# A step's order on TensorE in a linear-attention kernel: state inputs and weighted values right behind the projections, scores last, and the PSUM banks that go with it

## The reference

```python
h = _layernorm(x) * (1 + ca) + sa
q = elu(h @ Wq) + 1; k = elu(h @ Wk) + 1; v = h @ Wv      # 16 heads of 64
a = sigmoid(h @ Wa + ba + 2.0)
# per head, along the 2048 tokens:
S = a_t * S + k_t (outer) v_t;  z = a_t * z + k_t
out_t = (q_t . S) / (q_t . z + eps)
x = x + ga * (out @ Wo)
h = _layernorm(x) * (1 + cb) + sb
x = x + gb * experts(h)                                   # top 2 of 8, softmax weights
```

## Time and profile before

| | |
|---|---|
| median of 3 runs | 3618.65 us (3607.57 to 3626.08) |
| profiled execution | 3621.35 us, span 3619.6 us |
| granted TensorE clock, mean | 0.983 |
| PE busy | 3264.2 us, 90%, 51114 instructions |
| PEld busy | 2783.3 us, 77%, 51114 instructions |
| DVE busy | 2613.1 us, 72% |
| ACT busy | 1754.8 us, 48% |
| POOL busy | 1226.6 us, 34% |
| last scan of the attention phase (L915) | 2678.1 us |

### The profile page before, as it was taken

One profiled execution on the slowest core, in us unless ns is written; L12 is line 12 of the kernel. 1 busy time (PEld: TensorE's weight loads), 2 busy tenths in 40 slices (PEclk: granted clock), 3 DMA queues, 4 the chain that ended last, 5 costly groups with the idle time before them and its releaser, 6 DMA issues. The chain is left out here.

```text
span 3619.6 us, 129713 instructions
## 1 busy us (share of the span) xinstructions
PE 3264.2 (90%) x51114; PEld 2783.3 (77%) x51114; DVE 2613.1 (72%) x6866; ACT 1754.8 (48%) x4365; POOL 1226.6 (34%) x1057
## 2 busy tenths in 40 slices
PE   6898999999998998899999989989987999999998
PEld 5777777778787777777787777778775777777777
DVE  5676767666767767676666677767757888888887
ACT  4565656555665665555555666556542111111211
POOL 3333333343443333333333433333321222222222
PEclk9999999999999999999999999999998999999999
DMA  4222222222222222222222222222212111111110
GB/s 138 68 73 71 76 71 70 73 67 73 76 87 72 68 74 74 67 73 73 67 73 68 77 83 73 71 71 75 67 51 77 42 36 42 42 36 36 48 36 24
DMA packets 158631, 238.73 MB, mean 66 GB/s; under 512 B 30232, under 2 KB 82504, under 8 KB 157768
## 3 DMA queue, kind: packets, MB, share of 16 engines
q1 hardware_dynamic: 158024, 230.33, 19.8%
HBM read 194.58 MB, written 35.67 MB: 64 GB/s over the span
## 5 line engine op out<-in xcount | busy, mean ns | idle before, releaser
L442 POOL TENSOR_TENSOR oT_lo<-oT,oT_hi 128x512 fp32r<-128x512 f32 x256 | 332.0, 1297 | 1491.4 <-ACT oT_hi L526 1464.8
L543 ACT ACTIVATE kd_sb<-bank_scores,decay 128x64 f32<-128x64 f32 x2048 | 446.9, 329 | 655.0 <-PE bank_scores L741 652.6
L896 DVE SCALAR_TENSOR_TENSOR s_mid<-s_mid,lam_bc,bank_nums 128x65 f32<-128x65 f32 x1280 | 361.5, 282 | 46.9 <-DVE s_mid L896 1.4
L450 POOL TENSOR_TENSOR qs_sb<-lam_bc,qk_sb 128x512 f32<-128x512 f32 x256 | 333.9, 1304 | 157.1 <-PE bank_nums L725 119.5
L896 DVE SCALAR_TENSOR_TENSOR s_mid<-carry,lam_bc,bank_nums 128x65 f32<-128x65 f32 x256 | 72.3, 282 | 430.4 <-PE bank_dense L732 428.8
L741 PE MATMUL bank_scores<-qk_sb 64*64 64x128 f32 x8192 | 346.1, 274 | 29.5 <-issue 29.4
L508 ACT ACTIVATE qk_sb<-bank 128x512 f32<-128x512 f32 x512 | 318.0, 621 | 38.5 <-PE bank L582 21.3
L510 ACT ACTIVATE qk_sb<-qk_sb 128x512 f32<-128x512 f32 x512 | 324.2, 633 | 16.3
L915 DVE TENSOR_TENSOR_SCAN decay<-a_bc,eye 128x512 f32<-128x512 f32 x256 | 315.6, 1233 | 21.8 <-DMA a_bc<-rows_dram 21.8
L525 ACT ACTIVATE oT<-bank 128x512 f32<-128x512 f32 x256 | 153.1, 598 | 297.7 <-PE bank L707 297.1
L1247 DVE SCALAR_TENSOR_TENSOR acc<-bank_scores,comb,acc 128x256 f32<-128x256 f32 x512 | 230.7, 477 | 78.4 <-PE bank_scores L1161 77.5
(11 more groups left out here) (214 smaller groups left out, 9650.4 us busy)
## 6 DMA issues: line engine op xcount, KB each, us to landing
a_bc<-rows_dram SPq DMA_DIRECT2D x512, 128.0 KB, 2.9
lam_bc<-rows_dram SPq DMA_DIRECT2D x512, 128.0 KB, 2.9
x_in<-in_L_attn_x_dram SPq DMA_DIRECT2D x32, 512.0 KB, 6.3
x_res<-in_L_attn_x_dram SPq DMA_DIRECT2D x32, 512.0 KB, 3.9
x_dram<-x_res SPq DMA_DIRECT2D x32, 512.0 KB, 3.4
x<-x_dram SPq DMA_DIRECT2D x32, 512.0 KB, 3.3
out_dram<-x SPq DMA_DIRECT2D x32, 512.0 KB, 2.9
ew_raw<-in_L_ffn_expert_W_dram SPq DMA_DIRECT2D x8, 256.0 KB, 6.0
```

The costliest lines, as they stand in the source:

```text
L442: pool.tensor_tensor(oT_lo[:, u, :], oT32[:, :], oT_hi[:, u, :].bitcast(F32), ALU.subtract).then_inc(oT_lo_ready, 1)
L450: pool.tensor_tensor(qs_sb[:, na, :], lam_bc[na][:, :], q_sb, ALU.mult).then_inc(qs_ready, 1)
L543: ins = act.activation(kd_sb[:, t, hd * DH:(hd + 1) * DH], KTR[:, hd, t * CK:(t + 1) * CK], ACT.Copy, scale=decay[:, hd, t, CK - 1:CK])
L896: dve.scalar_tensor_tensor(dst, src, lam_bc[nb][:, (ch + 1) * CK - 1:(ch + 1) * CK], U[ch], ALU.mult, ALU.add).then_inc(state_step, 1)
```

## The change

**TensorE's order.** Behind the projections now stand inter, then the state inputs of all eight chunks in one piece, then the products of weighted scores and values, then the output's transposes (at u = 0 behind the dense jobs), then the dense jobs, and at the end the keys and scores of all eight chunks in one piece.

**Banks.** The state inputs of even chunks go to bank K, those of odd chunks to EXTRA's first bank. The output's transposes go to the first bank of SCORES (at u = 0 to DENSE), the h job's to DENSE and SCORES' second bank, both wo jobs to Q. So the state inputs wait for k_sb, the k projection for the state chain of the step before, and the scores for the copies of the transposed output.

**The other engines.** VectorE's state chain stands before the decay scan. ScalarE copies the transposed output before the dense evacuation (not at u = 0). GpSimd makes qs_sb before oT_lo. The dense jobs move: h from u = 1 to u = 0, wo behind it, v jobs a place forward or back; h_low goes from u = 1 to u = 0, the layer norm's application from u = 7 and 0 to u = 6 and 7, its statistics start at u = 2.

```diff
-DENSE_JOBS = {(0, 0): ("wo", -1, 1), (0, 1): ("v", 0, 5), (1, 0): ("v", 0, 6), (1, 1): ("h", 1, 0), (2, 0): ("v", 0, 7),
+DENSE_JOBS = {(0, 0): ("h", 1, 0), (0, 1): ("wo", -1, 1), (1, 0): ("v", 0, 6), (1, 1): ("v", 0, 7), (2, 0): ("v", 1, 0),
...
-        U_REST, DENSE = EXTRA[:, 0, :], EXTRA[:, 1, :]
+        U_ODD, DENSE = EXTRA[:, 0, :], EXTRA[:, 1, :]
-        HT = [U_REST, Q]
+        HT = [DENSE, SCORES[:, 1, :]]
+        U = [(K, U_ODD)[ch % 2][:, ch // 2 * VW:(ch // 2 + 1) * VW] for ch in range(NCK)]
+        def o_bank(u):
+            return SCORES[:, 0, :] if u else DENSE
...
 # GpSimd
-                if exists(T):
-                    pool.wait_ge(oT32_ready, n + 1)
-                    pool.wait_ge(oT_hi_ready, n + 1)
-                    pool.tensor_tensor(oT_lo[:, u, :], oT32[:, :], oT_hi[:, u, :].bitcast(F32), ALU.subtract).then_inc(oT_lo_ready, 1)
                     pool.tensor_tensor(qs_sb[:, na, :], lam_bc[na][:, :], q_sb, ALU.mult).then_inc(qs_ready, 1)
+                if u == 0 and exists(T + 1):
+                    for kt in range(KT):
+                        h_low(T + 1, 1 - s, kt)
+                if exists(T):
+                    pool.wait_ge(oT32_ready, n + 1)
+                    pool.wait_ge(oT_hi_ready, n + 1)
+                    pool.tensor_tensor(oT_lo[:, u, :], oT32[:, :], oT_hi[:, u, :].bitcast(F32), ALU.subtract).then_inc(oT_lo_ready, 1)
...
 # TensorE, step
-                    after(pe, oT_hi_ready, a - 3)
+                    after(pe, state_step, (a - 1) * NCK)
                     project(Ta, sa, pa, "wk", K, k_ps)
...
                 if exists(Tb):
+                    if exists(Ta):
+                        pe.wait_ge(k_ready, a + 1)
                     pe.wait_ge(kd_ready, b + 1)
...
-                    entering((NCK - 1,), u_last_ps)
+                    for ch in range(NCK):
+                        for hd in range(2):
+                            half, t = place(hd, ch)
+                            mm = pe.matmul(U[ch][rows[hd], :], kd_sb[rows[half], t, rows[hd]], v_sb[rows[half], t, v_col(pb, hd), :],
+                                           start=True, stop=True)
+                    mm.then_inc(u_ps, 1)
...
+                def transpose_o():
+                    if exists(T):
+                        if u:
+                            after(pe, kd_ready, free)
+                            after(pe, p_ready, free)
...
+                        after(pe, oT_hi_ready, n)
+                        pe.wait_ge(o_ready, n + 1)
+                        for t in range(NCH):
+                            mm = pe.transpose(o_bank(u)[:, t * CH:(t + 1) * CH], o_sb[:, t, :], ident[:, :])
+                        mm.then_inc(oT_ps, 1)
...
 # VectorE, step
+                if exists(Tb):
+                    chain(Tb, sb_, pb, b)
+                if exists(Ta):
                     after(dve, p_ready, a)
                     dve.wait_ge(a_loaded[na], (Ta * (PAIRS // 2) + pa // 2 + 1) * 32)
                     dve.tensor_tensor_scan(decay[:, :, :, :].rearrange("p h t i -> p (h t i)"), a_bc[na][:, :],
...
-                if exists(Tb):
-                    chain(Tb, sb_, pb, b)
```

More of the change, by code:

```diff
@@ L450, in step @@
                     pool.tensor_tensor(qs_sb[:, na, :], lam_bc[na][:, :], q_sb, ALU.mult).then_inc(qs_ready, 1)
-                if u == 7 and exists(T + 2):
+                if u == 0 and exists(T + 1):
[5 more added lines that the diff above has]
+                    pool.tensor_tensor(oT_lo[:, u, :], oT32[:, :], oT_hi[:, u, :].bitcast(F32), ALU.subtract).then_inc(oT_lo_ready, 1)
+                if u == 6 and exists(T + 2):
                     reciprocal_deviation(T + 2)
                     ln_apply(T + 2, (0, 1))
-                if u == 0 and exists(T + 1) and not leads(T):
-                    ln_apply(T + 1, (2, 3))
-                if u == 1 and exists(T + 1):
-                    for kt in range(KT):
-                        h_low(T + 1, 1 - s, kt)
+                if u == 7 and exists(T + 2):
+                    ln_apply(T + 2, (2, 3))
                 if leads(T) and u == 4:
@@ L601, in q_bank_free @@
                     pe.wait_ge(lam_row_ready, T + 2)
[L602 to L603 removed]
             def h_job(T):
[L606 removed]
+                after(pe, v_ready, T * 8 - 2)
+                after(pe, kd_ready, T * PAIRS - 5)
+                after(pe, p_ready, T * PAIRS - 5)
                 pe.wait_ge(xn_ready, T + 1)
@@ L633, in v_job @@
                 n = T * 8 + half * NCH + t
-                dst = Q if half == 1 and t == 1 else DENSE
+                dst = Q if half == 1 and t == 3 else DENSE
                 if half == 1 and t == 2:
-                    after(pe, wo_scaled, T * 2)
+                    pe.wait_ge(oT_hi_ready, T * PAIRS + 1)
+                    if exists(T + 1):
+                        pe.wait_ge(h32_ready, T * 2 + 3)
                 after(pe, v_ready, n)
@@ L687, in step @@
                 rows = [slice(i * CK, (i + 1) * CK) for i in range(2)]
+                free = a if exists(Ta) or not isinstance(Ta, int) else max(0, min(a, NG * PAIRS))
                 if exists(Ta):
@@ new lines, in step @@
+                if u:
+                    transpose_o()
+                dense_job(T, s, u, 0)
+                if dense_at(T, s, u, 1)[0]:
+                    if exists(Ta):
+                        pe.wait_ge(q_ready, a + 1)
+                    else:
+                        q_bank_free(T, u)
+                dense_job(T, s, u, 1)
+                if not u:
+                    transpose_o()
+                if exists(Ta):
+                    pe.wait_ge(k_ready, a + 1)
+                    pe.wait_ge(q_ready, a + 1)
+                    after(pe, kd_ready, a)
+                    after(pe, p_ready, a)
+                    if u and exists(T):
+                        pe.wait_ge(oT_hi_ready, n + 1)
+                    if u == 0 and exists(T + 1):
+                        pe.wait_ge(h32_ready, T * 2 + 4)
+                    if isinstance(Ta, int) and a == 0:
+                        pe.wait_ge(eye_ready, 1)
+                    pe.sem_inc(inputs_seen)
+                    for ch in range(NCK):
+                        eye_q = qk_sb[:, 0:2 * (ch + 1) * CK].rearrange("p (x i) -> p x i", x=2)[:, :, 0:CK]
+                        for hd in range(2):
+                            half, t = place(hd, ch)
+                            mm = pe.matmul(KTR_S[rows[half], hd, :, t, :], k_sb[rows[hd], ch * CK:(ch + 1) * CK], eye_q[rows[hd], :, :],
+                                           start=True, stop=True)
+                    mm.then_inc(s_ps, 1)
```

110 lines of the change are left out of this document (34 added, 76 removed).

## The result

| | before | after |
|---|---|---|
| median | 3619.9 us (3607.57 to 3626.08, 4 runs) | 3723.03 us (3713.13 to 3723.27, 4 runs) |
| ratio to before | | 1.0283, 95% interval 1.0264 to 1.0302 |
| profiled span | 3619.6 us | 3721.1 us |
| 28 groups in the middle | 2328.8 us | 2404.9 us |

The change costs 103 us or 2.8%. The sign and the mechanism were forecast; the size was not: 56 us. The measured time lies outside the forecast's own range (3645 to 3710) and inside the wide one (3600 to 3740).

What follows compares the result with a forecast made beforehand. TensorE's order was taken as the bound, losing waits and gaps. New waits 8.7, tile changes 1.9, removed wait -4.8, gaps -3.3, clock -0.7 gave +1.8 us per group: 3677 us, own range 3645 to 3710, 8 in 10 3600 to 3740.

Steps and rivals of the forecast that it cites:

- 8.7: TensorE's entering chunks waiting for k_sb: these waits together were to add 8.7 us per group.
- light step: Step with one v job (u = 4, 5, 6): 8.14 us before, forecast near 9.2 when steady.
- the meeting: VectorE's scan meets GpSimd's oT_lo and ends 1.07 us after it; loop from kd to kd 9.22 us.
- Rival 4: No change: the meeting happens in part of the steps, or a delay hides at u = 3 and 4; 3621 us, chance 0.12.
- rival 1: Faster: scan and oT_lo do not meet, loop 8.6 us, waits 5.2, sum -1.7 per group; 3568 us, chance 0.16.
- Rival 3: Slower: VectorE's clamp is caught by GpSimd's qs, loop 10.0 us in half of some five steps; 3736 us, chance 0.11.
- the term -3.3: Gaps on issue in TensorE's 64x64 runs: 3.3 of 3.5 us per group go, as shorter runs outlast code packets.
- rival 2: Slower: TensorE's gaps on issue stay; with half of 3.5 us left, sum 3.4 per group, 3727 us, chance 0.11.
- the sum of +1.8 us per group: All terms together: 8.7 + 1.9 - 4.8 - 3.3 - 0.7; over 31 groups +56 us.
- -0.7: Projections' share of the granted clock and shorter gaps on TensorE: about 1, half hidden in new waits, -0.7 us per group.
- two more changes of tile size: One more stretch of 64x64 tiles on TensorE: 0.35 us per step, less about 0.1; +1.9 us per group.

Runs made afterwards that it cites:

- e2: The changed kernel, but GpSimd's oT_lo also waits for the decay scan of the same step, so the two never run at once; 3600.92 us, ratio 0.9943.
- e1: The changed kernel with VectorE's order alone put back: decay scan ahead of the eight state updates; 3698.45 us, ratio 1.0217.
- e9: e7 with the transposes and the dense job ahead of inter at u = 3, 4, 5 and 7; 3505.61 us, ratio 0.9688.
- e7: e5 and e3 together, decay scan at the start of VectorE's step, k's projection no longer waiting for the state updates; 3496.97 us, ratio 0.9661.
- e3: The changed kernel, but the v job that goes to bank Q does not wait for the other v job's copy; 3688.40 us, ratio 1.0184.
- e4: The changed kernel with the edits of e2 and e3 together; 3568.59 us, ratio 0.9864.
- e5: The changed kernel with state inputs back in their earlier banks, seven chunks' behind the products, without the wait for k_sb; 3575.60 us, ratio 0.9875.

## Why the prediction was right in sign and mechanism, and half too small

**Right.** The wait of the transposes is gone and the entering chunks wait for k_sb; the medians are 0.27, 0.26, 0.26 us at u = 0 to 2, then 1.63, 0.43, 1.42, 2.03 and 1.31 (forecast 0.27 three times, 1.9, 1.1, 1.4, 2.0, 1.4, which add up to 8.6 and not to 8.7). At u = 4 the missing 0.6 is PE's wait for lam_row, which stands ahead of it in the same step. The light step u = 5 takes 9.35 us, forecast 9.2. The scan meets oT_lo in 209 steps and ends 1.08 behind it in each (1.076 to 1.087), forecast 1.07 from one event in the earlier trace rows; e2, which takes the meeting away, is 122 us faster. Rival 4, that it meets in part of the steps only or hides, is refuted by this too. The forecast's rival 1, the same kernel without the meeting, was to give 3568; e2 gives 3601, and its u = 1 still has the 0.94 us below. The Trainium skill (SBUF — State Buffer, section "SBUF: two separate sides") calls the two engines' common port pair an exclusive lock in which the second waits for the whole instruction, and gives about 115 ns from the lock's release to the end for a DMA of GpSimd's that had waited for VectorE; the trace agrees with the lock in both directions (scan behind oT_lo, in e1 qs behind the scan), and has 1.08 us from the first's end to the second's, of the 1.215 or 1.29 that the second takes alone: most of it runs only then.

Rival 3 (clamp caught by qs) is refuted for the changed kernel: 303 to 310 ns in all 120 clamps, qs 0.16 behind. It is what e1 shows: 1220 ns in all 120 clamps, and 10.0 us steps, the length that the rival had.

The gaps on issue are gone (5.4 us in 7 of them left), as the term -3.3 had it, and with them rival 2's condition. That the rivals' 3727 and 3736 lie nearer to the measured 3723 than the forecast is chance. The reason given for the term is not confirmed. For it speaks that all 63 gaps over 0.6 us among the small matmuls of the kernel before (28 groups) end 1.19 to 1.57 us (median 1.36) after a code packet has landed, worked out from the DMA records, and that these packets start 0.4 to 1.6 us ahead of the gap but for one, 0.1 behind its start, all of them inside the run of small matmuls. Packets come every 7.4 us (median), so a fixed distance in all 63 is hardly chance. Three of them, us:

```
packet starts  packet landed  PE stops  PE resumes  resumes behind packet
338.75         340.11         339.51    341.55      1.44
422.88         424.14         423.88    425.59      1.45
451.19         452.14         452.82    453.44      1.30
```

So they are most likely waits for code. Against the run's length as the whole cause stand three counts: in runs of 128 at u = 4 and 5 e9 has 3 gaps over 0.6 us where the kernel before has 17; the kernel before has none at u = 0, 1 and 7, whose runs are as long, and 24 at u = 2; and e7 has 10 at u = 3 and 4 in and behind runs of 96. Where the packet boundaries fall in the code differs from kernel to kernel, and I can't move them at will; that stays open.

**Wrong: the sum of +1.8 us per group, which was 2.7 in the middle groups, and more at the start.** What it left out:

- *The v_ready wait at u = 1.* "u = 0 has h and wo and u = 1 a second v, which hide the loop". They do, but the second v job, into another bank, kept the wait for the copy of the first: 0.69 us idle, 0.94 in the step, x 31 = 29 us. e3 measures 35. The forecast counted the job and not its wait.
- *The clock.* "The projections' share of the granted clock of 0.99" was the only place where the forecast spoke of it, as a gain and a part of its -0.7. The gain did not come. Worked out from the clock records of both traces, TensorE runs at 1.2 GHz for 30.7 us of the 28 groups in the kernel before and for 30.7 us in the changed one; only the place is another. Before, these stretches stand behind gaps on issue (seven of 1.8 to 2.5 us, one of 3.5). In the changed kernel u = 6 waits 2.03 us for k_sb, and in 7 of 28 groups the step then takes 11.3 to 11.7 us, against 9.9. Two such waits, and the 3.2 us behind each:

```profile
310.60 0.36 PE L734 MATMUL bank<-v_sb,kd_sb 64*64 64x65 f32 x2 [2.02 <-DVE qk_sb L918]
```

```profile
396.52 0.27 PE L734 MATMUL bank<-v_sb,kd_sb 64*64 64x65 f32 x2 [2.02 <-DVE qk_sb L918]
```

```profile
310.60:313.80 3.20, 3.20 (x70) 3.08 (x71) 2.03 (x8) 0.04 (x1) 1.27 (x1) 0.51 0.02 5
396.52:399.72 3.20, 3.17 (x83) 2.93 (x83) 2.67 (x10) 1.09 (x3) 1.40 (x2) 1.00 0.02 5
```

The same wait, and once 0.51 of the clock, once 1.00. It costs 7 x 1.4 / 28 = 0.35 us per group. In e3 it strikes 16 of 28, which is why u = 6 got longer there; in e2, e4, e5 and e7, whose waits at u = 3 to 6 are 1.7 us at most, none. Ahead of the 28 groups the clock does make a difference: from the first k matmul on, 19.4 us at 1.2 GHz against 6.8, at most 6 us of time.
- *The start.* The first k projection starts at 45.5 us, before at 40.4: the new table has a third v job ahead of it, and the first v matmul, which needs the low halves of wv, starts at 34.0 us instead of 31.9. Of the other 11.6 us up to n = 16, up to 6 are the clock's; the step n = 1 alone, with a gap on issue of 1.62 us and 1.2 GHz behind it, is 3.0 longer.

Together: in the 28 groups 0.92 us per group is missing, and the v wait is 0.94 of it. The other terms cancel there. The waits for k_sb, in the view of the weight loads in which the forecast had read the removed wait, come to 8.1 us per group (the view puts them down to issue), and the wait for lam_row adds 0.6, against 8.7:

```profile
PEld bank L734 <- issue: 227.0, 223, 2.4
```

The two more changes of tile size are right by e9. What became of the -0.7, whose share of the clock did not come, no run shows by itself. Outside the 28 groups 20 us are missing (25.4 measured, 3 x 1.8 forecast): 5 are the later start, 5 the v wait in five more steps, up to 6 the clock; some 4 stay open.

As the runs show it, the change's idea, the order on TensorE, was sound: e5, which keeps it but for the state inputs' banks and the place of seven of them, is 1.2% faster than before, and e4, which keeps it wholly, is 1.4% faster. Its cost came from the wait for k_sb that goes with state inputs in k's bank, and from oT_lo, which now starts just ahead of the scan, since VectorE's order puts the scan behind the updates.

## What to carry to other kernels

When an order is changed on the engine that bounds, look which pairs of instructions of VectorE and GpSimd now start within each other's span: a single wait on the one with more idle time was worth 122 us. Before a tile moves into another one's bank, list what must have been read there, and ask when that is ready, not how long the wait is now: in k's bank every delay of VectorE went straight into TensorE's step. And of each job that is moved beside another, carry its waits with it, not only its work.
